# A four-layer graph network on one core: edge features loaded from ScalarE's queue, fewer SyncE instructions per group, and a dense stage in halves with filler matmuls

## The reference, cut to what matters

```python
edge_index = jnp.stack([src, dst])
x = _layernorm(x + gat(x, src, dst))            # two attention convolutions, 4 heads
x = _layernorm(x + gcn(x, edge_index, edge_weight))   # three weighted convolutions, concatenated
x = _layernorm(x + segment_sum(x[src], dst))
x = _layernorm(x + egnn(x, edge_index, edge_attr_32)) # two convolutions, each with a batch norm

def _gat_conv(x, src, dst, W, al, ar, b, act):
    z = (x @ W).reshape(N, H, F)
    e = leaky_relu((z * al).sum(-1)[src] + (z * ar).sum(-1)[dst], 0.2)
    alpha = softmax of e over the edges of one dst
    return act(segment_sum(z[src] * alpha[..., None], dst) + b)

def _batchnorm(x, gamma, beta):
    mu = jnp.mean(x, axis=0)
    var = jnp.var(x, axis=0)
    return (x - mu) * jax.lax.rsqrt(var + EPS) * gamma + beta
```

## Time and profile before

| what | value |
|---|---|
| median of 3 runs | 7297.76 us (7267.9 to 7310.4) |
| the profiled execution's own time | 7296.74 us |
| its span | 7295.1 us |
| busy: PE / DVE / ACT / POOL | 62% / 57% / 29% / 47% |
| mean granted clock of TensorE | 0.741 of full speed |

### The profile page before, as it was taken

How to read it: one execution, slowest core, us unless ns; L and a number is a source line. 1 busy time by engine, 2 the same in 40 slices (tenths; PEclk the granted TensorE clock), 3 DMA queues, 4 the chain that set the end, 5 groups by cost and what they waited for, 6 DMA issues and landing times.

```text
span 7295.1 us, 121057 instructions
## 1 busy us (share of the span) xinstructions
PE 4543.0 (62%) x28553; PEld 2993.0 (41%) x28553; DVE 4165.7 (57%) x13273; ACT 2134.5 (29%) x5938; POOL 3458.1 (47%) x4137
## 2 busy tenths in 40 slices
PE   1565666666566565444555555555578888888865
PEld 1233333333333344222222322333377777677754
DVE  4677677687787663666566676667661111224344
ACT  0444355454454431333333333333310000000000
POOL 2777767777677603777777777777500000000000
PEclk9676667676776665666666666666659999999988
DMA  5455455455555532444444544444439899899966
GB/s 93 128 147 157 123 155 160 140 155 157 139 156 146 151 99 56 118 128 121 129 127 121 136 135 131 129 133 134 138 138 415 356 396 416 340 416 399 371 284 251
DMA packets 934340, 1390.68 MB, mean 191 GB/s; under 512 B 483496, under 2 KB 689474, under 8 KB 917769
## 3 DMA queue, kind: packets, MB, share of 16 engines
q1 hardware_dynamic: 687776, 912.42, 36.9%
q0 software_dynamic: 128976, 222.12, 12.3%
q10 hardware_dynamic: 117332, 253.47, 9.3%
HBM read 1014.16 MB, written 373.27 MB: 190 GB/s over the span
## 4 chain that ended last, share of the span: by engine, by line
issue 23%; SPq 18%; DVE 16%; PE 15%; DMA 14%; DVEq 5%; ACT 4%; another core or an unknown queue 2%; POOL 2%; ACTq 1%; POOLq 0%
DMA arena<-adj_w_d 8%; SPq L520 4%; DMA arena<-adj_c_d 4%; SPq L499 4%; DVE arena L1020 3%; SPq L486 3%; PE bank L1756 3%; PE bank L1757 3%; PE bank L1760 2%; PE bank L1718 2%; ACT arena L1891 2%; POOL arena L800 2%; SPq L501 2%; DVE arena L1043 1%
## 5 line engine op out<-in xcount | busy, mean ns | idle before, releaser
L800 POOL DMA_INDIRECT arena<-table_d,arena x3136 | 3135.1, 1000 | 1353.6 <-issue 1125.6
L1612 PE MATMUL bank<-arena 128*128 128x500 f16 x3750 | 1355.4, 501 | 1109.3 <-issue 639.4
L1633 PE MATMUL bank<-arena 128*65 128x40 f32 x7500 | 742.5, 255 | 880.4 <-issue 667.6
L1612 PEld LDWEIGHTS bank<-arena 128*128 128x128 f16 x3750 | 431.3, 123 | 1826.5 <-issue 1561.4
L1891 ACT ACTIVATE arena<-arena 128x128 f16<-128x128 f16 x3750 | 1122.7, 396 | 85.0 <-DVEq L1121 55.3
L1633 PEld LDWEIGHTS bank<-arena 128*65 128x65 f32 x7500 | 671.2, 169 | 1022.6 <-issue 851.2
L1756 PE MATMUL bank<-arena 125*128 125x250 f16 x3750 | 859.3, 274 | 156.1 <-DMA arena<-adj_w_d 132.9
L1757 PE MATMUL bank<-arena 125*128 125x250 f16 x3750 | 855.5, 273 | 0.0
L1020 DVE TENSOR_SCALAR arena<-arena 128x500 f16<-128x500 f16 x1875 | 689.0, 367 | 214.7 <-issue 118.6
L1614 PE MATMUL bank<-arena 128*128 128x500 f16 x1875 | 681.6, 471 | 68.6 <-issue 66.3
L1106 DVE SCALAR_TENSOR_TENSOR arena<-arena,bank 128x250 f16<-128x250 f16 x1250 | 455.3, 411 | 441.2 <-issue 330.3
(11 more groups left out here) (244 smaller groups left out, 4326.2 us busy)
## 6 DMA issues: line engine op xcount, KB each, us to landing
arena<-adj_w_d SPq DMA_DIRECT2D x720, 625.0 KB, 10.9
arena<-adj_c_d SPq DMA_DIRECT2D x345, 625.0 KB, 11.5
adj_w_d<-arena ACTq DMA_DIRECT2D x125, 1250.0 KB
arena<-msg_d SPq DMA_DIRECT2D x1250, 103.5 KB
msg_d<-arena POOLq DMA_DIRECT2D x196, 552.0 KB
adj_c_d<-arena ACTq DMA_DIRECT2D x125, 625.0 KB
arena<-table_d,arena POOLq DMA_INDIRECT x3136
arena<-in_edge_features SPq DMA_DIRECT2D x625, 51.0 KB
```

The costliest lines, as they stand in the source:

```text
L800: g_.indirect_dma_start(ring[:, i, k * XC:(k + 1) * XC], None, table_d, bass.IndirectOffsetOnAxis(ap=idx_cur[:, i, k:k + 1], axis=0)).then ...
L1612: mm(wb, lhsT=row_oh[:, slot, c, i, :], rhs=col_oh[:, slot, c, :], start=(c == 0 and i == 0), stop=(c == CH - 1 and i == 1))
L1633: last = mm(out, lhsT=rows_sl[:, g, w, c, 0:AGG], rhs=grh[:, g, w * CH + c, :], start=(c == 0), stop=(c == CH - 1))
```

## The change

**Window stages.** SyncE no longer loads edge features; ScalarE does (`features`), between the evacuation of the former group's last adjacency block and the wait for `logits_made`, in group 0, 1, 2 of a round (layer 0) and 0, 2 (layer 1). The starts and the need of a group now lie side by side (`group_row`), so that one read gives both, and the read made for the records of a group is kept for its message rows. The `er` values are spread for groups 0 and 1 together, and for 2, 3 and 4 together (`spread`), each after a wait for `logits_made`; VectorE waits for them by `er_loaded`. In the preparation the two rows become DMAs with pieces of five values and of one.

**Attention dense stage.** `keep_busy` puts 6 float16 matmuls of 128x500, whose result is overwritten, ahead of the head products of each batch, 12 ahead of the first of a layer.

**Convolutions.** The scale of convolution 0 comes from a bound (the largest of 50 values per partition, times the root of 64) in place of the maximum over all 3200, and so is made before the layer norm; that of convolution 5 from a bound out of the batch norm's factors, made before `gat_vector(d, 1)`. The layer norms ahead of convolution 0 and at the end, the batch norms' scale and shift, and the final store go half by half. The batch norms' sums and sums of squares are gathered block by block in `post`; `batch_norm_factors` then works on 64 elements only, and scale and shift are one multiply and one add.

```diff
+        group_row = lists[:, 0:NGR * (WG + 1)].rearrange("p (g k) -> p g k", k=WG + 1)
...
             def records(b, x):
 
-                wait_reg(sp, rec_used[x], b + layer * B)
                 if x in ADJ[layer]:
                     wait_reg(sp, adj_used[x], b)
+                else:
+                    wait_reg(sp, rec_used[x], b + layer * B)
                 offs = offsets(mybir.EngineType.SP, b, x)
                 for w in range(WG):
                     sp.dma_start(rec_sl[:, x, w, :], edge_rows(rec_d, offs[w])).then_inc(rec_loaded[x], 16)
-                    if x in ADJ[layer]:
-                        sp.dma_start(ef_sl[:, built_before(layer, x), w, :], edge_rows(a["edge_features"], offs[w])).then_inc(adj_loaded[x], 16)
+                return offs
+
+            def spread(b, g):
+
+                k = ER_PART[g]
+                before = b * NG + (NGR * layer + g + k - NG)
+                if not (isinstance(before, int) and before <= 0):
+                    wait_reg(sp, s("logits_made"), before)
...
                     if g + AHEAD < NG:
-                        records(b, g + AHEAD)
+                        known[g + AHEAD] = records(b, g + AHEAD)
...
-                    blocks = sp.value_load(need_row[0:1, bass.ds(b * (NG * WG) + g * WG + WG - 1, 1)], min_val=1, max_val=NBLK)
-                    wait_reg(sp, s("msg_ready"), blocks + layer * NBLK)
+                    if g in ER_PART:
+                        spread(b, g)
+                    offs = known[g] if g in known else offsets(mybir.EngineType.SP, b, g)
+                    wait_reg(sp, s("msg_ready"), offs[WG] + layer * NBLK)
...
-                    offs = offsets(mybir.EngineType.SP, b, g)
...
+        def parts_half(d, n, x_in, t):
+
+            up = scl[0:NT, n, 0:1]
+            v.tensor_scalar(x_one[:, t, 0:F], x_in[:, t, :], up, None, ALU.mult)
+            d.drain()
+            v.scalar_tensor_tensor(x_one[:, t, F:2 * F], x_in[:, t, :], up, x_one[:, t, 0:F], ALU.mult, ALU.subtract)
+            d.drain().then_inc(s("x_hl"), 1)
...
-                    v.tensor_reduce(stat[:, 5, :], x_out[:, t2, :].rearrange("p t f -> p f t"), AX.X, ALU.add)
...
+                    v.tensor_tensor(yc, x_out[:, t2, :], bc(stat[:, 6, :], 1, 2), ALU.subtract)
                     d.drain()
-                    v.tensor_tensor(stat[:, 0, :], stat[:, 0, :], stat[:, 5, :], ALU.add)
+                    v.tensor_tensor(yd[:, 0:2, :], yc, yc, ALU.mult)
+                    v.tensor_tensor(yd[:, 2, :], yc[:, 0, :], yc[:, 1, :], ALU.add)
+                    d.drain()
+                    v.tensor_tensor(yd[:, 0, :], yd[:, 0, :], yd[:, 1, :], ALU.add)
+                    v.tensor_tensor(stat[:, 7, :], stat[:, 7, :], yd[:, 2, :], ALU.add)
+                    d.drain()
+                    v.tensor_tensor(stat[:, 5, :], stat[:, 5, :], yd[:, 0, :], ALU.add)
                     d.drain()
...
-            d.drain()
-            v.tensor_tensor(z, z, bc(stat[:, 1, :], 1, T), ALU.subtract)
-            d.drain()
-            v.tensor_tensor(sq, z, z, ALU.mult)
-            d.drain()
-            v.tensor_reduce(stat[:, 0, :], sq.rearrange("p t f -> p f t"), AX.X, ALU.add)
...
+        def batch_norm_half(d, z, t):
+
+            v.tensor_tensor(z[:, t, :], z[:, t, :], bc(stat[:, 4, :], 1, TH), ALU.mult)
+            d.drain()
+            v.tensor_tensor(z[:, t, :], z[:, t, :], bc(stat[:, 1, :], 1, TH), ALU.add)
             d.drain()
...
-            layer_norm(d)
-
-            v.tensor_tensor(xin, x_sb, bc(dinv, 2, F), ALU.mult)
-            d.drain()
+            top_scale(d, 0)
+            for h in halves(0):
+                t = half(h)
+                layer_norm(d, t)
+                v.tensor_tensor(xin[:, t, :], x_sb[:, t, :], bc(dinv[:, t], 2, F), ALU.mult)
+                d.drain()
+                parts_half(d, 0, xin, t)
...
-            batch_norm(d, hout, 0)
-            parts_vector(d, 5, hout)
+            batch_norm_factors(d, 0)
+            for h in halves(5):
+                batch_norm_half(d, hout, half(h))
+                parts_half(d, 5, hout, half(h))
...
+            for h in range(2):
+                t = half(h)
+                batch_norm_half(d, xin, t)
+                v.tensor_tensor(x_sb[:, t, :], x_sb[:, t, :], xin[:, t, :], ALU.add)
+                d.drain()
+                layer_norm(d, t)
+                d.sem_inc(s("cv_done"), 1)
...
+        def keep_busy(out, count):
+
+            for _ in range(count):
+                mm(out[:, 0:T * WN], lhsT=iota_lo, rhs=iota_key, start=True, stop=True)
...
                 wait_some(pe, s("gat_y"), i * NG + (u + base - 1))
+                keep_busy(gat_banks(u)[0], 12 if first(i) and u == 0 else 6)
...
+            def features(b, x):
+
+                wait_some(act, adj_used[x], b)
+                offs = offsets(mybir.EngineType.Activation, b, x)
+                for w in range(WG):
+                    act.dma_start(ef_sl[:, built_before(layer, x), w, :], edge_rows(a["edge_features"], offs[w])).then_inc(adj_loaded[x], 16)
...
                     evacuate(b, todo[0] - 1)
+                    for x in ADJ[layer]:
+                        if g == built_before(layer, x) * (1 + layer):
+                            features(b, x)
                     act.wait_ge(s("logits_made"), b * NG + (ng + g + 1))
```

More of the change, by code:

```diff
@@ L326, in build @@
         rows_loaded = [sem(f"rows_loaded{i}") for i in range(NG)]
+        er_loaded = {g: sem(f"er_loaded{g}") for g in (0, 2)}
         top_stored = [sem(f"top_stored{i}") for i in range(2)]
@@ L411, in halves, with half @@
             return (0, 1) if way(n) > 0 else (1, 0)
+        def half(h):
+            return slice(h * TH, (h + 1) * TH)
         def block_of(n, i, u):
@@ L439, in prep_sync @@
             sp.dma_start(ptrb, ptr_d.to_broadcast([NT, NW + 1])).then_inc(s("ptr_back"), 16)
-            sp.dma_start(ptr_row[:, 0:NW], ptri_d[:, 0:NW]).then_inc(s("ptr_back"), 16)
-            sp.dma_start(need_row, need_d).then_inc(s("ptr_back"), 16)
+            with nc.allow_non_contiguous_dma(reason="starts and needs by group"):
+                sp.dma_start(group_row[:, :, 0:WG], ptri_d[:, 0:NW].rearrange("o (g k) -> o g k", k=WG)).then_inc(s("ptr_back"), 16)
+                sp.dma_start(group_row[:, :, WG:WG + 1], need_d.rearrange("o (g k) -> o g k", k=WG)[:, :, WG - 1:WG]).then_inc(s("ptr_back"), 16)
             sp.wait_ge(s("table_made"), 1)
@@ L486, in offsets @@
             return nc.values_load_multi_w_load_instructions(
-                ptr_row[0:1, bass.ds(b * (NG * WG) + g * WG, WG)], engines=(engine,), min_val=0, max_val=EP - CAP,
-                skip_runtime_bounds_check_because="a start is a count of edges of at most E = 200000, and E + CAP is below EP")[1]
+                flat(group_row)[0:1, bass.ds(b * (NG * (WG + 1)) + g * (WG + 1), WG + 1)], engines=(engine,), min_val=0, max_val=EP - CAP,
+                skip_runtime_bounds_check_because="a start is a count of edges of at most E = 200000, and E + CAP is below EP; a need is a count of blocks")[1]
         def win_sync(sp, layer):
             def records(b, x):
-                wait_reg(sp, rec_used[x], b + layer * B)
                 if x in ADJ[layer]:
                     wait_reg(sp, adj_used[x], b)
+                else:
+                    wait_reg(sp, rec_used[x], b + layer * B)
                 offs = offsets(mybir.EngineType.SP, b, x)
@@ L750, in _ @@
                 conv_sync(sp, n)
-            sp.wait_ge(s("cv_done"), 7)
-            sp.dma_start(nodes(a["out"]), x_sb).then_inc(s("out_stored"), 16)
-            sp.wait_ge(s("out_stored"), 16)
+            for h in range(2):
+                sp.wait_ge(s("cv_done"), 7 + h)
+                sp.dma_start(nodes(a["out"])[:, half(h), :], x_sb[:, half(h), :]).then_inc(s("out_stored"), 16)
+            sp.wait_ge(s("out_stored"), 32)
         def consts_pool(pool):
@@ L1142, in win_vector @@
                         d.sem_inc(rec_used[x], 1)
+                    if g in ER_PART:
+                        d.wait_ge(er_loaded[g], b * 16 + 16 * (layer * B + 1))
                     d.wait_ge(rows_loaded[g], b * ROWS + ROWS * (layer * B + 1))
@@ L1485, in conv_vector @@
                     former = block_of(n, i, u) - way(n)
-                    post(former, 1 - u % 2, k - 1)
+                    post(former, 1 - u % 2, k - 1, first(i) and u == 1)
                     if n < 3:
@@ L1762, in top_scale_tensor @@
         def top_scale_tensor(pe, n):
-            if n in (3, 4):
+            if n >= 3:
                 return
-            k = n if n < 3 else 3
+            k = n
             pe.wait_ge(s("top_x"), 2 * k + 1)
@@ L2030, in conv_scalar @@
                 act_(x_two[:, t, :], x_one[:, t, :], ACT.Copy, scale=1.0 / LOW).then_inc(s("x_low"), 1)
+                if n == 0 and at_ == 0:
+                    std_scalar(act, half(halves(0)[1]))
             def transposed(k):
@@ L2064, in _ @@
```

(7 more changed lines are left out.)

128 lines of the change are left out of this document (77 added, 51 removed).

## The result

The changed kernel takes 7217.74 us (median of 5 runs, 7210.36 to 7237.76) beside 7297.76 us (7267.9 to 7313.21, 5 runs) of the kernel before: a ratio of 0.9889 with a 95% interval of 0.9865 to 0.9913. Forecast were 7236 us and "faster"; the time came out 18 us under it. The profiled execution has a span of 7208.7 us, against 7295.1.

A forecast was written before the change was run, and what follows sets the result against it. It took layer 0 as a loop of VectorE, TensorE and ScalarE, layer 1 as GpSimd's gathers, the dense stages as TensorE. Terms -5 + 1 - 15 - 2 - 8 - 19 - 14 = -62 gave 7236 us, 8-in-10 range 7180 to 7292.

The forecast's parts named there:

- Ahead of convolution 0: Before convolution 0: first half starts TensorE early, second piece begins at 5437.1 in place of 5445.0; -8 us.
- Between convolutions 4 and 5: Batch norm before convolution 5: factors on 64 elements, then work by halves, shorten TensorE's wait; -19 us.
- The end: Final batch norm, layer norm and store: factors 5.5 us, then halves, only the second half's store follows; -14 us.
- the first dense stage: After layer 0's attention: fillers hold TensorE's clock up, batches shorten, less twelve cold fillers; -15 us.
- 0.59 x 5.50: First dense stage: a batch's own 5.50 us shrink by the transposes' clock ratio; with fillers 4.65 us a batch.
- the second stage: Dense stage after layer 1: fillers bring TensorE's batch to 3.9 us, VectorE then about as slow; -2 us.
- SyncE, whose queue the change relieves, is on that chain nowhere that I can see: Layer 0: VectorE, TensorE and ScalarE hand small pieces to each other; SyncE's queue does not hold them back.
- I take 2 and 3 us: SyncE's relieved queue gains 2 us in layer 0 and 3 us in layer 1's tail, together -5 us.
- the sign of its rivals: Layer 0's length: more than 20 us away from 2508 us would point to a rival explanation.
- Rival (c): Layer 0 was held by SyncE and falls to layer 1's gather pace: -54 us, 7182 us; chance 0.10.
- rival (d): ScalarE's feature loads come late and VectorE waits, in a quarter of layer 0's loading groups: +70, 7306 us; chance 0.06.
- The window part: Attention group loops and preparation: -5 us from SyncE's relieved queue, ScalarE's loads 0, preparation DMAs +1 us.

The follow-up runs named there:

- fill_f32: Kernel before plus all of the change but the window part, fillers made of float32 128x128 matmuls: 7324.43 us, ratio 0.9921.
- no_fill: The whole change, with a group's need checked on SyncE, but without the filler matmuls, against the kernel before: 7180.2 us, ratio 0.9979.
- late_read: Kernel before plus the window part with need check, a group's starts read once more behind the waits: 7347.79 us, ratio 0.9976.
- read_only: Kernel before plus the window part's single checked read; er spread group by group, feature loads on SyncE: 7362.7 us, ratio 0.9985.
- windows_only: Kernel before plus the whole window part, with a group's need checked against its bounds on SyncE: 7227.35 us, ratio 1.0044.
- before_again: The kernel before, unchanged, run once more with a profile: 7198.94 us in one run.
- sync_lean: Kernel before plus the window part with need check, but feature loads left on SyncE: 7229.26 us, ratio 1.0048.

## Why the prediction was right, and where it was not

**Right in mechanism and near in size:** the convolutions' edits, as the traces' starts show them. Ahead of convolution 0 -9.3 for -8: the first piece starts early, the second waits for VectorE's second half, as worked out. Between convolutions 4 and 5 -17.6 for -19, with the stretch to the next batch norm counted in. The end -16.6 for -14, because the factors take 4.4 us (6950.90 to 6955.26) and not 5.5; the second half's store took 10 us, as assumed.

**Mis-sized:** the first dense stage, -22 for -15. The term was "0.59 x 5.50" for a batch; the head products, two thirds of it, halved (3.62 to 1.86), and the batch came to 4.17 us and not 4.65. In the second stage -0.5 for -2, VectorE being the slower one, as said. The clock rose as forecast, but not for the reason given: the prediction chose it because float16 had 1.00 where float32 alone had 0.50, and float32 fillers of 128x128 lift it too (fill_f32). no_fill shows that the fillers did it; here the right term rested on a wrong reason.

**The step that failed** is in the first part: "SyncE, whose queue the change relieves, is on that chain nowhere that I can see", and with it "I take 2 and 3 us". Layer 0 gave 42 us in the recorded traces, past the 20 us that the prediction had set as the sign of its rivals. I read VectorE's waits, saw the loop of three engines and asked no further why it was slow. The queues' own rows show what I missed: SyncE's and TensorE's instructions stood still between one another without a wait. In the changed kernel SyncE has 784 such stalls in the stretch where it had 987, and TensorE's weight loads 488 where they had 691. SyncE stalls about as often per instruction, 0.17 against 0.15, and has fewer instructions (4627 against 6421). Rival (c) had the place and nearly the size (-54); whether SyncE's stalls or TensorE's hold the layer, no run separates. Nor is it shown that fewer instructions on SyncE make fewer stalls on TensorE: late_read has 740 on SyncE but 635 on TensorE's weight loads, as many as read_only. Stalled traces of one layer 0 program in one comparison differ by 19 us (2618 and 2599), so the 42 of a single pair is uncertain by about as much.

**What the forecast could not see:** where there are no stalls, the window part costs 31 us (between the traces of windows_only and before_again 26: 2 in the preparation, 14 in layer 0, 14 in layer 1's gathers, -3 behind them). It is not rival (d), since ScalarE's loads alone measure 0.9999. In layer 1 the price lies in GpSimd's own instructions, which the sum had as unchanged; in layer 0 they account for 8 of the 14. In the recorded comparison the same shows as +13.3 in layer 1. So the forecast of -62 is 18 short of the recorded -80 and 38 beyond the -24 of the regime without stalls. The terms of the dense stages and convolutions were good, -58 forecast and -62.4 in the traces. The window part was not: -4 forecast, -24 in the recorded traces, +31 without stalls. That the sum came near is luck to that extent, since which regime the comparison would meet was not in the reasoning.

**Open:** what switches the stalls on; whether the single read or what comes with it is what costs the 31 us (by exclusion only); what makes the clock fall in some executions of the second dense stage; and the +3.4 us of convolutions 0 to 4. They take 1561.0 in the changed kernel and 1557.6 before.

## What to carry to other kernels

Before a stage is called a loop of engines, look whether their queues stand still ahead of instructions that wait for nothing; if so, the same change may be worth something else on a run without it. A relief of SyncE is no gain where GpSimd sets the pace, and this one cost 31 us there. Filler matmuls paid in the stage where TensorE is the slower engine (22 us net, for 1.3 us a batch). Where another engine makes TensorE wait they brought 0.5 us, and in one execution, in which the clock fell, they cost 30: there they are better left out. Without stalls the best kernel measured is the one with the dense part alone, 0.9927; whether it also beats the whole change with stalls was not run side by side.

## What the runs showed of the hardware

The same program on the same chip took 7196 us in one comparison and 7371 us in another. The traces put most of the difference in layer 0 (136 us more there in read_only, with stalls, than in the all but equal sync_lean, without). In the slower ones SyncE stood 0.7 us on average ahead of 740 to 1080 instructions a layer, and TensorE's weight loads 0.8 us in 606 to 641 places of layer 0. The Trainium skill (TensorE: Matmul & The Clock Gate, Part 1, What's actually happening) has activity release the throttle; the fillers agree with that. By that sentence alone the first dense stage, 97% busy before the change, should have been at full clock, and it stood at 0.50; with fillers of either type it had 0.83 to 0.88. And GpSimd's gathers took 1.30 us on average beside VectorE's 128x600 additions in windows_only, and 0.96 beside its float16 products.
